# Eight batches of a quantised decoder layer on one core: attention weights turned by transposing DMA transfers, and four stages pipelined anew

## The reference

```
h   = layernorm(x) * q(gamma) + q(beta)
qkv = floor8(floor8(h) @ q(w_qkv))              # 3 x 1024 columns, 16 heads of 64
d   = floor8((q k^T) * temp)                    # per head 512 x 512
a   = floor8(softmax(d))                        # per head 512 x 512
o   = floor8(floor8(a @ v) @ q(w_out))
x1  = layernorm(x + o)
s   = clip((x1 Wq + bq)(ctx Wk + bk)^T / sqrt(32), +-1e4)   # 16 heads of 32
x2  = layernorm(x1 + (softmax(s) (ctx Wv + bv)) Wo + bo)
out = layernorm(x2 + ffn(x2))                   # int8-rounded 512 -> 2048 -> 512, gelu, rank-16 terms
```

## Time and profile before

| | us |
|---|---|
| median of 3 runs (lowest to highest) | 3690.12 (3690.01 to 3691.11) |
| the profiled execution, its own time | 3690.49 |
| its span in the profile | 3688.7 |
| PE busy | 2745.9 (74%) |
| DVE busy | 2574.5 (70%) |
| ACT busy | 1463.6 (40%) |
| POOL busy | 146.4 (4%) |

### The profile page before, as it was taken

One profiled execution on the slowest core, in us unless ns is written; L12 is line 12 of the kernel. 1 busy time (PEld: TensorE's weight loads), 2 busy tenths in 40 slices (PEclk: granted clock), 3 DMA queues, 4 the chain that ended last, 5 costly groups with the idle time before them and its releaser, 6 DMA issues. The chain is left out here.

```text
span 3688.7 us, 46276 instructions
## 1 busy us (share of the span) xinstructions
PE 2745.9 (74%) x13160; PEld 1067.8 (29%) x13160; DVE 2574.5 (70%) x4657; ACT 1463.6 (40%) x2397; POOL 146.4 (4%) x148
## 2 busy tenths in 40 slices
PE   1189999566664666664599969999995645999998
PEld 1134322111111433331244412222222223444443
DVE  6877799989887988884355547777773576455444
ACT  0000444489887988871122224444441001212221
POOL 0000333000000000000000000000001210000000
PEclk8599999555555989887799969999997877999999
DMA  5221221223232443434544433323325531001000
GB/s 199 74 91 46 92 116 78 103 102 112 100 105 90 135 126 125 129 111 183 193 165 166 175 86 84 84 75 82 86 63 194 182 121 35 24 23 36 33 23 23
DMA packets 199676, 375.20 MB, mean 102 GB/s; under 512 B 23680, under 2 KB 109696, under 8 KB 187136
## 3 DMA queue, kind: packets, MB, share of 16 engines
q1 hardware_dynamic: 195344, 357.03, 29.5%
q10 hardware_dynamic: 4208, 16.78, 1.2%
HBM read 218.02 MB, written 155.71 MB: 101 GB/s over the span
## 5 line engine op out<-in xcount | busy, mean ns | idle before, releaser
L1289 DVE TENSOR_REDUCE stats<-bank 128x1024 f32 (+1 forms) x352 | 407.9, 1216 | 65.5 <-PE bank L765 32.0
L1154 ACT ACTIVATE arena<-arena,scale 128x512 bf16<-128x512 int8 x512 | 410.1, 802 | 103.1 <-DVE arena L1476 94.4
L825 PE MATMUL bank<-arena 64*128 64x512 bf16 x512 | 306.2, 605 | 173.9 <-DVE arena L1471 138.8
L1583 DVE TENSOR_REDUCE arena<-bank 128x2 f32<-128x1024 f32 x256 | 312.8, 1222 | 136.3 <-PE bank L926 136.3
L1471 DVE CUSTOM_DVE_ANT_0 arena<-bank,arena,fac 128x512 int8<-128x512 f32 x512 | 353.9, 747 | 38.3 <-issue 17.8
L1169 ACT ACTIVATE arena<-arena,scale 128x512 f32<-128x512 int8 x512 | 366.4, 801 | 27.9 <-DVE arena L1497 14.8
L1235 ACT ACTIVATE arena<-bank 128x1024 f32<-128x1024 f32 x256 | 248.2, 1021 | 322.5 <-PE bank L942 322.5
L973 PE MATMUL bank<-arena 128*32 128x512 f32 x2048 | 272.0, 607 | 40.8 <-issue 32.7
L765 PE MATMUL bank<-arena 128*128 128x512 bf16 x1024 | 246.7, 386 | 59.9 <-DVE arena L1419 52.4
L845 PE MATMUL bank<-identb,arena 128*128 128x128 bf16 x2048 | 155.9, 237 | 172.1 <-DVE arena L1506 171.7
L1267 ACT ACTIVATE arena<-bank,arena,fac 128x512 f32<-128x512 f32 x128 | 99.5, 777 | 456.2 <-PE bank L1097 456.2
(11 more groups left out here) (189 smaller groups left out, 3585.1 us busy)
## 6 DMA issues: line engine op xcount, KB each, us to landing
dq_scr<-arena SPq DMA_DIRECT2D x128, 256.0 KB, 2.0
arena<-dq_scr SPq DMA_DIRECT2D x128, 256.0 KB, 2.7
arena<-half_scr SPq DMA_DIRECT2D x256, 128.0 KB, 2.8
qkv_scr<-arena SPq DMA_DIRECT2D x8, 3072.0 KB, 9.7
arena<-in_x SPq DMA_DIRECT2D x16, 1024.0 KB, 7.0
arena<-qkv_scr SPq DMA_DIRECT2D x128, 128.0 KB, 2.2
o_scr<-arena SPq DMA_DIRECT2D x64, 256.0 KB, 2.9
arena<-o_scr SPq DMA_DIRECT2D x8, 2048.0 KB, 9.2
```

The costliest lines, as they stand in the source:

```text
L825: return mm(dst, qE[r, h // 2, P * t:P * t + P], kE[r, h // 2, :], start=True, stop=True)
L1154: last = A(e_dump[:, NT * (h % 2) + t, :], dq8[:, h % 4, t, :], ACT.Exp, bias=negm_b[:, par, c:c + 1], scale=scale[:, S_DOTS:S_DOTS + 1], ...
L1289: return V.tensor_reduce(dst, src, ax, ALU.max, apply_absolute_value=True)
L1583: V.tensor_reduce(mxX[:, mp, hs, 2 * u:2 * u + 2], bank[:, 0:2, :], AX.X, ALU.max).then_inc(S("sX_red"), 1)
```

## The change

- **Stage 6.** DVE writes the negated maxima for two heads at once (ACT is released for both), copies a batch's maxima and sums (`keep_rows`) after head 5 of the following batch, and runs `through` all batches without the wait at their ends.
- **Stage 7.** The 16 PE transposes per head and DVE's move out of PSUM go. SP issues one `dma_start_transpose` per head (128 partitions x 2048 bf16, SBUF to SBUF) from `aG` into `aTG`; both have four buffers. The 129 is taken off at the outputs: PE multiplies v by a column of ones once per batch (`sum_values`, 32 one-column matmuls), ACT scales those sums by -129 (`sums_kept`) and adds them as a bias when it moves a pair out (`pair_out`). All engines run `through` the batches; the next batch's row factors are copied in the middle of a batch.
- **Stage 10.** The maxima are turned before the last quarter of the group before, into one of two `nmT`; clips of half the size at two places; the split of the maxima in two halves. The row sums are inverted group by group: SP stores them, loads them spread over 128 partitions (`load_spread`), DVE inverts 16 columns (`invert`), SP stores and loads them four times broadcast (`load_rec`), POOL multiplies the group's values (`divide`) before `store_group`. Wo, bo and the first two batches' values and x1 are loaded before the last four groups' transfers.
- **Stage 11.** No division and no broadcast loads; values of batch b + 2 are loaded as soon as PE has finished batch b; x1 of batch b + 2 after x2 of batch b is stored.

The diff, cut to its core:

```diff
+        def through(e, body):
+            body(0, 0)
+            with e.Fori(0, NB // 2 - 1) as j:
+                body(j * 2 + 1, 1)
+                body(j * 2 + 2, 0)
+            body(NB - 1, 1)
...
-        aG = cG(BF16, 2, NT, T)
-        aTG = cG(BF16, 2, NT, T)
+        aG = cG(BF16, 4, NT, T)
+        aTG = cG(BF16, 4, NT, T)
...
+            def turn_weights(b, h):
+                sp.wait_ge(S("aG_done"), b * (H * NT) + 8 + NT * h + NT)
+                hold(sp)
+                if not (is_batch(b, 0) and h < 4):
+                    sp.wait_ge(S("pvG_mm"), b * H + 16 + h - 4 + 1)
+                hold(sp)
+                r = h % 4
+                sp.dma_start_transpose(aTG[:, r].rearrange("p t q -> p (t q)").rearrange("p (c q) -> p c q", q=P),
+                                       aG[:, r].rearrange("p t k -> p (t k)")).then_inc(S(f"head_moved{r}"), 16)
...
                     elif more:
                         load_dq(b + 1, h + 4 - H)
+                    turn_weights(b, h)
                     if h % 2 and h >= 5:
                         store_o(b, (h - 5) // 2)
+                    elif h % 2 and not is_batch(b, 0):
+                        store_o(b - 1, PAIRS + (h - 5) // 2)
...
             def group_dma(i, r):
...
+                if not (known and i < 2):
+                    store_rec(i - 2)
+                if not (known and i < 3):
+                    store_group(i - 3, (r + 1) % 2)
+                if not (known and i < 1) and not (known and i == GROUPS - 1):
                     store_sums(i - 1, (r + 1) % 2)
-                if not (isinstance(i, int) and i < 2):
-                    store_group(i - 2, r % 2)
+                if not (known and i < 2):
+                    load_rec(i - 2, r % 2)
+                if not (known and i < 1) and not (known and i == GROUPS - 1):
+                    load_spread(i - 1, (r + 1) % 2)
...
+            def sum_values(b, par):
+                pe.wait_ge(S(f"vG_in{par}"), b * 8 + 16 - 8 * par)
...
+                for p in range(PAIRS):
+                    for j in range(NT):
+                        last = mm(bank[:, par, p:p + 1], vG[:, par, j, P * p:P * p + P], ones_g[:, 0:1],
+                                  start=j == 0, stop=j == NT - 1)
+                last.then_inc(S("vsum_mm"), 1)
+            def values(b, par):
+                sum_values(b, par)
+                for h in range(H):
+                    values_of_head(b, par, h)
+            through(pe, values)
...
+            def pair_out(b, par, p):
+                act.wait_ge(S("pvG_mm"), b * H + 16 + 2 * p + 2)
+                act.wait_ge(S(f"oG_stored{p % 2}"), b * 64 + 16 * (p // 2) + 16)
...
+            def sums_kept(b, par):
+                act.wait_ge(S("vsum_mm"), b + 1)
+                A(vsum_g[:, par, :], bank[:, par, 0:PAIRS], ACT.Copy, scale=-129.0).then_inc(S("vsum_ready"), 1)
             def weigh(b, par):
+                for s in range(H):
+                    if s == 2:
+                        sums_kept(b, par)
...
+                    if s % 2 and not (is_batch(b, 0) and s < 3):
+                        pair_out(b, par, (s - 3) // 2)
...
+            def invert(i):
+                dve.wait_ge(S("sums16_in"), i * 16 + 16)
+                V.reciprocal(sums16, sums16).then_inc(S("rec_done"), 1)
             def group(i, r):
                 for c in range(NT):
                     for u in (0, 1):
                         if not (isinstance(i, int) and i * G + c + LEAD >= NB * H):
                             max_pair(i * G + c + LEAD, (r + (c + LEAD) // G) % 2, (c + LEAD) % G, u)
+                        if c == 0 and not first:
+                            clip(i - 1, 1 - r, NT - 1, u)
+                        if c == 1:
+                            clip(i, r, 0, u)
+                        if (c, u) == (2, 0):
+                            clip(i, r, 1, None)
+                        if (c, u) == (2, 1) and not last:
+                            split_max(i + 1, 1 - r, True, False)
+                        if (c, u) == (3, 0) and not last:
+                            split_max(i + 1, 1 - r, False, True)
+                        if (c, u) == (3, 1):
+                            clip(i, r, 2, None)
+                        if (c, u) == (0, 1) and not (isinstance(i, int) and i < 2):
+                            invert(i - 2)
...
+            def after_batch(b, par):
+                sp.wait_ge(S("wo_mm"), b * NT + NT)
+                hold(sp)
+                load_values(b + 2, par)
+                store_x2(b, par)
+                sp.wait_ge(S(f"x2_stored{par}"), b * 8 + 32 - 8 * par)
+                load_x1(b + 2, par)
```

More of the change, by code:

```diff
@@ L48 @@
 ENGINES = 5
+TURNED = 16 + 16 * NB * H // 4
 STAGES = (1, 2, 3, 5, 6, 7, 8, 9, 10, 11, 12, 13)
@@ L225, in decoder @@
             "rs_tile": H * NT,
-            **{f"dq_stored{s}": 16 for s in range(4)},
+            **{f"head_moved{s}": 16 for s in range(4)},
         }
@@ new lines, in store_rec, with load_rec @@
+            def store_rec(i):
+                sp.wait_ge(S("rec_done"), i + 1)
+                hold(sp)
+                sp.dma_start(spread(rec_scr, i), sums16).then_inc(S("rec_stored"), 16)
+            def load_rec(i, par):
+                sp.wait_ge(S("rec_stored"), i * 16 + 16)
+                hold(sp)
+                for g in range(G):
+                    row = rec_scr[i, g:g + 1, :] if isinstance(i, int) else rec_scr[bass.ds(i, 1), g, :]
+                    sp.dma_start(recB[XD * g:XD * g + XD, par, :], row.broadcast_to([XD, T])).then_inc(S(f"rec_in{par}"), 16)
@@ L858, in _ @@
-            batches(pe, values)
+            def sum_values(b, par):
+                pe.wait_ge(S(f"vG_in{par}"), b * 8 + 16 - 8 * par)
+                if is_batch(b, 0):
+                    pe.wait_ge(S("row_cols"), 1)
+                else:
+                    pe.wait_ge(S("vsum_ready"), b)
+                hold(pe)
+                for p in range(PAIRS):
[3 more added lines that the diff above has]
+                last.then_inc(S("vsum_mm"), 1)
@@ new lines, in values_of_head @@
+            def values_of_head(b, par, h):
+                pe.wait_ge(S(f"head_moved{h % 4}"), TURNED + b * 64 + 16 * (h // 4) + 16)
+                if h % 2 == 0:
+                    pe.wait_ge(S("oG_evac"), b * PAIRS + h // 2 + 1)
+                hold(pe)
+                r = 64 * (h % 2)
+                for j in range(NT):
+                    last = mm(bank[r:r + DH, 4 + (h // 2) % 4, :], vG[:, par, j, DH * h:DH * h + DH],
+                              turned_g[:, h % 4, :, j, :], start=j == 0, stop=j == NT - 1)
+                last.then_inc(S("pvG_mm"), 1)
@@ L941, in take_max @@
                     q = slice(XD * g, XD * g + 3)
-                    last = mm(bank[:, 2 + g, :], ones_b[q, :], nmT[q, :], start=False, stop=True)
+                    last = mm(bank[:, 2 + g, :], ones_b[q, :], nmT[q, r % 2, :], start=False, stop=True)
                     if g % 2:
@@ L988, in group @@
                         values_of(i - 1, (r + 1) % 2, c, 0)
+                    if c == NT - 1 and not (isinstance(i, int) and i == GROUPS - 1):
+                        turn_max(i + 1)
                     key_scores(i, r, c, 0)
@@ L1177, in _ @@
+            through(act, weigh)
+            pair_out(NB, 0, -1)
             barrier(act, 7)
@@ L1520, in _ @@
+            link(V.memset(ones_g, 1.0))
+            row_factors(0, 0)
+            through(dve, floor_weights)
+            pair_peak(NB, -2)
+            pair_peak(NB, -1)
             dve.wait_ge(S("oG_peak"), 2 + NB * PAIRS)
@@ new lines, in split_max, with clip @@
+                ch.n = 3
+                if second:
+                    ch.link(V.tensor_tensor(by_tile(restX), by_tile(negX), slots[:, :, :, 0], ALU.subtract))
+                    ch.link(V.tensor_copy(slots[:, :, :, 1], by_tile(restX)))
+                    V.tensor_tensor(slots[:, :, :, 2], by_tile(restX), slots[:, :, :, 1], ALU.subtract).then_inc(S("nm_ready"), 1)
+                    ch.end()
+            def clip(i, r, c, a):
+                heads = slice(0, G) if a is None else slice(2 * a, 2 * a + 2)
+                n = 2 if a is None else 1
+                dve.wait_ge(S("eX_done"), i * 8 + 2 * c + (a or 0) + n)
+                e = eT[:, r, heads, c, :]
+                V.tensor_scalar(e, e, CLIP_FLOOR, 1.0, ALU.max, ALU.min).then_inc(S("clipped"), n)
@@ L1613, in group @@
+            def invert(i):
+                dve.wait_ge(S("sums16_in"), i * 16 + 16)
+                V.reciprocal(sums16, sums16).then_inc(S("rec_done"), 1)
             def group(i, r):
+                first, last = (isinstance(i, int) and i == k for k in (0, GROUPS - 1))
                 for c in range(NT):
```

314 lines of the change are left out of this document (142 added, 172 removed).

## The result

| | before | changed |
|---|---|---|
| median of the runs (lowest to highest), us | 3690.61 (3690.01 to 3693.8) | 3834.03 (3829.93 to 3839.96) |
| the profiled execution / its span, us | 3690.49 / 3688.7 | 3836.0 / 3834.1 |
| ratio to before, 95% interval | 1 | 1.0385 [1.0372, 1.0398] |

The change makes the kernel 143 us slower, where I had forecast 43. The first thing to read is again the table of windows, one per changed stage, which answers to the earlier trace rows. Each window is laid just inside the stage, so its length is not quite the stage's; the columns are length, busy time (and instructions) of PE, PEld, DVE, ACT and POOL, granted clock as a share of 2.4 GHz, DMA share and GB/s.

A forecast was written before the change was run, and what follows sets the result against it. It took ACT to bound stages 6 and 7 and PE stage 10, with stage 11's PE busy only 119 of 209 us. Sum: 3690.5 - 47 + 67 + 100 - 77 = 3733.5 us; range 3590 to 3970.

The forecast's parts named there:

- stage 10, +100: Stage 10: DVE's wait for the inverted sums lengthens a group from 19.30 to 23.5 us; +100 us, bounds +75 to +140.
- 9.4 in all, then PE's turn ..., 1.7, and 0.3: Stage 10: after the sums land at 12.1 us, DVE's steps, PE's work and SP's waking end the group at 23.5 us.
- without anything else a group would take about 17.8 us: Stage 10: PE's rest of 1.30 us goes and turning moves forward, so a group without the new wait takes 17.8 us.
- Stage 7, +67: Stage 7: batch ends -53, transposing transfers +108 and the wait of `sums_kept` +12; bounds -53 to +300.
- Batch ends -53: Stage 7: ACT's rests of 7.6 us at each of seven batch ends go, worth 53 us.
- The transposes, +108: Stage 7: transposing transfers make a head take 4.0 us in place of ACT's 3.16, over 128 heads +108 us.
- two bounds: Stage 7, per head: 3.15 us if turned bytes cost what plain ones do; 4.5 or 11.5 if transfers stand alone.
- The wait of `sums_kept`, +12: Stage 7: ACT waits 2 to 6 us per batch for 32 small matmuls taking 2.4 to 5 us; +12 us.
- Stage 6, -47: Stage 6: ACT sets the pace at 3.30 us per head without rests at batch ends, 433 against 480 us; -47.
- the bound of -55: Stage 6: the most that could be gained, from ACT's 421.9 us busy plus the start; about -55 us.
- Stage 11, -77: Stage 11: PE starts at the barrier and paces at 14.9 us per batch, plus 13, against 209 us; -77.
- clock still high: Stage 10: named sign that the clock stays high although DVE waits and a group takes 23.5 us.

The follow-up runs named there:

- experiment 7: Experiment 4's kernel with stage 10's maxima split whole at one place and turned by PE after the last quarter's key scores: 3455.16 us.
- experiment 10: Changed kernel, transposing transfers kept, with experiment 1's list order and the maxima split whole, turned after the last quarter's scores: 3592.82 us, ratio 0.9732.
- experiment 2: Changed kernel with only store_group moved ahead of load_stacks in stage 10's transfer list: 3835.78 us, ratio 1.039.
- experiment 3: Changed kernel with store_rec, store_sums, load_rec and load_spread moved ahead of load_stacks and store_group left last: 3746.47 us, ratio 1.0148.
- experiment 4: Experiment 1's kernel with stage 7's turning by PE transposes again, two buffers, still run through the batches: 3512.15 us, ratio 0.952.
- experiment 5: Changed kernel with each transposing transfer moving only half of a head's bytes, the other half left zero: 3725.85 us, ratio 1.0087.
- experiment 1: Changed kernel with stage 10's list reordered: store_rec, store_group, store_sums, load_rec, load_spread first, load_v and load_stacks last: 3654.55 us, ratio 0.9899.
- experiment 8: Experiment 4's kernel with POOL's multiply by the reciprocals in stage 10 done on 8 of 512 columns only: 3469.95 us, ratio 0.9394.

## Why the prediction was wrong in size

The direction was right and each stage moved the way it was forecast; the sum was 100 us short, nearly all of it in the term **stage 10, +100**, which measured +205.5.

*Stage 10.* The mechanism was right: DVE's reciprocal waits for `load_spread`, queued on SP behind the eight stack loads; forecast 6.9 us, measured 6.27, released by `arena<-sums_scr`, landing 11.35 us after SP's first issue where 12.1 was worked out. The step that failed is the one behind it: "9.4 in all, then PE's turn ..., 1.7, and 0.3", 11.4 us from the landing to the group's end. In the group shown it measured 2532.49 - 2516.53 = 16.0. I had added DVE's durations as if DVE never waited again; before PE's next turn at 2530.21 it waits for PE four more times, 3.5 us in all. Another 0.8 us are DVE's own steps (a half clip takes 0.82 us from start to start, where I had halved the whole one to 0.57), and 0.3 the end. PE is late because it had rested itself, 2.95 and 2.37 us, and was then at the lower of its two clock levels (granted 0.52 from 2518.04 to 2524.88): two score matmuls of L986, two of L994, then L1002, L1030, L986 and L1030 take 6.84 us there, and the same row of instructions took 3.81 from 2503.55 to 2507.36. That is 3.0 us, read from rows; no run changed the clock by itself.

Over the stage, the steady list of 26 groups measured 26 x (26.4 - 19.35) = +183, where +109 was forecast. The six other groups, taken as -9, measured +22: in the last three DVE's reciprocal still waits 3.4, 2.7 and 5.1 us, although no stack loads stand ahead of it. Even without them the list needs 4.7 us from `load_v` to `load_spread` (2963.61 to 2968.34), most of it the store of the reciprocals and their loads.

The two windows, before and changed:

```profile
2400.00:2500.00 100.00, 91.15 (x607) 21.79 (x605) 78.50 (x94) 48.55 (x58) 0.00 (x0) 1.00 0.28 79
```

```profile
2400.00:2500.00 100.00, 75.52 (x420) 16.09 (x417) 56.13 (x74) 33.80 (x40) 5.04 (x4) 0.81 0.26 69
```

A second sentence failed with it: "without anything else a group would take about 17.8 us". With both waits for transfers gone a group took 20.3 on average, because the halved split and the earlier turn put a new rest of about 2.2 us in front of PE. The change has removed PE's 1.30 us and put a longer one elsewhere; only the order of experiments 7 and 10 gives the 17.9.

That ACT's wait for `store_group` costs nothing beside DVE's and about 3 us per group alone was right (experiments 2 and 3).

*Stage 7, +67, measured +86.* Batch ends -53, measured -55. The transposes, +108 at 4.0 us per head, measured +141 at 4.3. I had placed the value between two bounds for SP's order and waits; what runs showed is the transfer engines' own time, 1.00 busy, with a head's turned bytes at some 3 us in place of 1.7 at the plain rate. The wait of `sums_kept`, +12, measured almost nothing: ACT waits for PE's L899 1.8 us in all, because the 32 small matmuls take 1.0 us (at 1406.51) and not 2.4 to 5. The Trainium skill (Advanced Engine Details and Errata, X-Bar Transpose (TRN2)) has transposing transfers as fast as plain ones; experiments 4 and 5 say otherwise for this shape. The figure of the Trainium skill's page DMA: Bandwidth & Descriptors (Latency and other measured facts), 261 GB/s, which I had turned into 2.0 us, is nearer, and still above the 175 to 185 GB/s measured.

*Stage 6, -47, measured -63.* The mechanism was right, the size was not. ACT's exp in the changed kernel:

```profile
L1211 ACT ACTIVATE arena<-arena,scale 128x512 bf16<-128x512 int8 x512 | 408.1, 799 | 53.5 <-DVE arena L1559 53.5
```

Of the 53.5 us of idle time 51.1 lie before the stage's first exp, so ACT rests 2.4 us in the whole stage. From its first exp to its last ACT takes 409.9 us (703.6 to 1113.5), where it took 475.2 (701.4 to 1176.6). I had read one batch end and taken its 4 us for all seven; the next one in the same trace is

```profile
822.44 0.81 ACT L1154 ACTIVATE arena<-arena,scale 128x512 bf16<-128x512 int8 x1 [9.17 <-DVE arena L1476]
```

and they alternate: 3.99, 9.17, 4.00, 9.30, 4.00, 9.36, 4.00, together 43.8 us and not 28. The other 21.5 us were small gaps within the batches: a head now takes 3.20 us, and I had kept 3.30. So the bound of -55, worked out from the 421.9 us of busy time, was none.

*Stage 11, -77, measured -86.* PE starts at 3033.43, 5.4 us after its last matmul of stage 10, the barrier between them (where before it rested 35.82), POOL is absent, and the stage is PE's 111.7 of 127.

Of the signs I had named, "clock still high" in stage 10 was the one that came out wrong (0.84). The sum kept the full clock through a stall of 6.9 us, and two rows at hand spoke against that: PE's work of 17.5 us in a group of 23.5 leaves 6 us of rests, and the earlier trace rows had PE at a clock of 0.50 in stage 6, where it was busy 306 of 481 us.

## What to carry to other kernels

In a queue that is served in order, put the small transfers of the latency chain ahead of any that waits for the end of the group; here the order of seven calls was worth 180 to 216 us. When a stall is put into a steady loop, price what comes after it too: the engines behind it rest in turn, PE can run on at its lower clock, and hand-overs that were hidden show up, so the loop's new time is not the stall added to the old durations. A transposing transfer that replaces work of a PE with time to spare moves it to the transfer engines; here it cost there about 1.8 times what the same bytes cost plainly (an estimate: 3.0 us against 524 KB at 312 GB/s, 1.7), and PE's granted clock for what was left was 0.50 in place of 0.99 (experiment 4). And read more than one turn of a loop before its number goes into a sum: the batch ends of stage 6 alternate between 4 and 9 us, and the groups of experiment 1 vary between 19.4 and 21.4.

## What the runs showed of the hardware

- A transposing transfer of 128 x 2048 bf16 within SBUF goes as about 2,100 packets of 250 bytes and takes the 16 engines some 3 us, 175 to 185 GB/s; the stage's plain traffic before went at 312. SP, which issues it, is held by it; two in the changed kernel's trace:

```profile
1301.03 2.90 SPq L512 DMA_TRANSPOSE arena<-arena  x1
...
1304.85 2.76 SPq L512 DMA_TRANSPOSE arena<-arena  x1
```

  One of half the bytes (experiment 5) mostly holds it 1.24 us.
- A POOL multiply of 128 x 512 stretched a DVE cast of 128 x 16 from 0.20 to 1.18 us: it began 0.14 us before the cast, and both ended within 0.06 us (experiment 1; 1.31 us in experiment 4, where it began 0.01 us before). The maximum read from PSUM beside it kept its 1.23 (experiment 7). The Trainium skill (SBUF — State Buffer, Who interferes with whom) has a port pair that VectorE and GpSimd share, held by whichever starts first for its whole instruction, with casts among those that can need it and reductions not; by that rule, this case's rows agree.
- PE's level of clock (1.2 or 2.4 GHz) after a rest, by the time that its matmul pairs took: .59 to .61 after rests of 0.44 (experiment 7), 1.2 (thirteen groups of experiment 8) and 1.3 us (before); after single rests of 2.1 to 2.3 us .59 in some groups and .64 to 1.06 in others (experiments 1 and 4); and 1.03 to 1.04 after the second of two rests of 2.0 us or more in a row (nine groups of the changed kernel from 2300 to 2520). In stage 7 the granted clock was 0.50 with PE busy 248 of 548 us and 0.99 with it busy 271 of 400.
